# A two-layer graph network on one core: the first dense layer summed in half chunks, one norm shared between two engines, and the branch moved ahead of the stores' wait

## The reference

```python
h = relu(LN(x))
for l in 1, 2, 3:                      # SAGE, mean over incoming edges
    agg = segment_sum(h[src], dst) / count(dst)
    h = agg @ Wl.T + bl + h @ Wr.T     # relu after layers 1 and 2
x = x + h
h = relu(LN(x))
m = gelu((h[src] + edge_attr) @ We1 + be1) @ We2 + be2
u = (1 + eps) * h + segment_sum(m, dst)
x = x + gelu(u @ Wu1 + bu1) @ Wu2 + bu2
```

## Time and profile before

| what | value |
|---|---|
| median of 3 runs | 880.73 us (879.21 to 881.85) |
| profiled execution, its own time | 879.47 us |
| its span, first to last instruction | 877.3 us |
| PE busy | 826.8 us (94%), 4876 matmuls |
| DVE busy | 694.9 us (79%) |
| ACT busy | 323.8 us (37%) |
| POOL busy | 379.7 us (43%) |
| mean granted clock of PE | 0.969 |

### The profile page before, as it was taken

The page is one execution under the profiler, slowest core; times in us unless marked ns, Lnnn a source line. Parts: engine busy times, 40 slices in busy tenths (PEclk is TensorE's granted clock), DMA queues, the critical chain, the costliest instruction groups (busy, mean ns, idle before and its releaser), DMA issues.

```text
span 877.3 us, 16376 instructions
## 1 busy us (share of the span) xinstructions
PE 826.8 (94%) x4876; PEld 632.6 (72%) x4876; DVE 694.9 (79%) x1887; ACT 323.8 (37%) x570; POOL 379.7 (43%) x439
## 2 busy tenths in 40 slices
PE   3688999999999999999899999999999999999995
PEld 1243555555687787778677888888887898888884
DVE  8999999998355444454799989988979997997981
ACT  3566677776255555544211111121121112112111
POOL 1000000000022222232477777777777777777771
PEclk9569999999999999999799999999999999999998
DMA  4301011001000000011573443444443453444431
GB/s 112 120 2 13 3 15 13 14 3 15 11 1 0 1 1 12 13 32 40 131 197 106 128 137 109 134 137 149 138 139 93 147 149 94 147 138 140 128 87 33
DMA packets 38403, 67.61 MB, mean 77 GB/s; under 512 B 15178, under 2 KB 25893, under 8 KB 38054
## 3 DMA queue, kind: packets, MB, share of 16 engines
q1 hardware_dynamic: 27302, 43.95, 17.0%
q0 software_dynamic: 11008, 22.57, 9.8%
HBM read 63.18 MB, written 3.30 MB: 76 GB/s over the span
## 4 chain that ended last, share of the span: by engine, by line
PE 79%; DVE 12%; POOL 4%; issue 2%; DMA 1%; ACT 1%; SPq 0%; ACTq 0%; DVEq 0%
PE f_ps L1414 20%; PE f_ps L1359 16%; PE f_ps L1456 11%; PE f_ps L1352 10%; PE f_ps L1400 8%; POOL f_adj L678 4%; PE f_ps L1257 3%; PE f_ps L1250 2%; PE f_ps L1326 2%; DVE f_region L747 2%; DVE f_region L745 2%; PE f_ps L1396 1%; PE f_ps L1288 1%; DVE f_region L751 1%; DVE f_region L749 1%
## 5 line engine op out<-in xcount | busy, mean ns | idle before, releaser
L678 POOL DMA_INDIRECT f_adj<-table,f_by_edge x344 | 327.9, 953 | 105.8 <-issue 102.8
L970 DVE TENSOR_SCALAR f_select<-f_ps 128x512 fp32r<-128x512 f32 x425 | 261.0, 678 | 9.0 <-PE f_ps L1414 8.1
L1414 PE MATMUL f_ps<-f_select,f_pair 125*128 125x512 f32 x850 | 220.1, 407 | 4.5 <-DVE f_select L970 4.5
L663 POOL CAST f_wide<-f_adj 125x500 fp32r<-125x500 uint8 (+1 forms) x70 | 40.4, 577 | 358.5 <-ACT f_adj L1122 212.6
L1414 PEld LDWEIGHTS f_ps<-f_select,f_pair 125*128 125x128 f32 x850 | 156.7, 191 | 42.6 <-issue 7.1
L1236 ACT ACTIVATE f_adj<-f_adj 128x512 f32<-128x512 f32 (+1 forms) x88 | 55.1, 626 | 295.5 <-DVE f_adj L1092 259.1
L1359 PE MATMUL f_ps<-f_wide,f_pair 125*128 125x500 f32 (+1 forms) x700 | 162.5, 385 | 1.5 <-DVE f_wide L802 0.6
L1122 ACT CAST f_adj<-f_ps 128x500 f32 x213 | 125.9, 591 | 55.8 <-PE f_ps L1257 43.3
L1359 PEld LDWEIGHTS f_ps<-f_wide,f_pair 125*128 125x128 f32 x700 | 122.2, 189 | 33.5 <-issue 6.2
L1352 PE MATMUL f_ps<-f_adj,f_parts 125*128 125x500 fp8e4 (+1 forms) x525 | 128.7, 354 | 0.0
L1456 PEld LDWEIGHTS f_ps<-f_adj 128*128 128x128 f32 x984 | 119.4, 192 | 10.0 <-issue 9.2
(11 more groups left out here) (149 smaller groups left out, 716.0 us busy)
## 6 DMA issues: line engine op xcount, KB each, us to landing
f_region<-in_edge_attr_T SPq DMA_DIRECT2D x33, 768.0 KB
f_adj<-table SPq DMA_DIRECT2D x512, 0.5 KB
f_adj<-table,f_by_edge POOLq DMA_INDIRECT x344
f_src_rows<-in_src_row SPq DMA_DIRECT2D x16, 256.0 KB, 3.5
f_xT<-in_xT SPq DMA_DIRECT2D x1, 1562.5 KB, 6.6
f_adj<-inv SPq DMA_DIRECT2D x1, 1562.5 KB, 7.5
out<-f_xT SPq DMA_DIRECT2D x6, 250.0 KB, 3.0
table<-f_region SPq DMA_DIRECT2D x6, 224.0 KB
```

Source lines behind the costliest of these rows:

```text
L678: pool.indirect_dma_start(out=rows[:, r % RW, j * D:(j + 1) * D], out_offset=None, in_=table, in_offset=bass.IndirectOffsetOnAxis(ap=table ...
L970: ins = dve.tensor_scalar(select[:, u % SELECT, :], offset, float(b * NP - CENTRE), None, ALU.is_equal)
L1414: ins = pe.matmul(z_columns(g), chosen[0:NP, p, b, :], select[0:NP, u % SELECT, :], start=b == 0 and p == 0, stop=b == NB - 1 and p == 1, ...
```

## The change

- Each chunk of layer 1 except 0 and 6 is summed as two halves of 250 columns, each with 75 matmuls. A half may begin two slots after its own columns are filled (`half_group`: 36; 53, 70; 87, 104; 121, 138; 155, 172; 189, 206; 212). The second half need not wait for a new PSUM region.
- `rate`: 2.8 full-width units a slot before slot 80, then 2.3. The units of chunk 0 now lie in slots 38 to 64, chunk 1 in 64 to 93, 2 in 94 to 126, 3 in 126 to 159, 4 in 159 to 191, 5 in 191 to 216, 6 in 216 to 218. Full-width equivalents behind the build: 45.25 (before 81.75).
- `ready` is 24 + 5c, six slots sooner, for `norm0`, `turn`, `high` and the rest of the splitting.
- `norm0` of chunks 1, 3, 5 goes from DVE to ACT (one activation for each block, with the ReLU).
- `variance(c)` on PE also waits for the square root of the chunk before.
- Five more tiny comparisons in the check of the inputs (`small`).
- SP no longer waits for the stores inside the block; the semaphores are cleared by POOL after the flag is loaded, without the second barrier; SP waits for the stores and clears their semaphore behind the branch.

```diff
-        self.build_group = last(self.EP * self.DT)
+        self.build_group = last(self.EP * self.DT, self.node_end)
+        self.half_end = [[e for e in (self.cols(c)[0] + self.NBC // 2 * self.NP, self.node_end[c]) if c and e < self.node_end[c] or e == self.node_end[c]]
+                         for c in range(self.NC)]
+        self.half_group = [last(self.EP * self.DT, ends) for ends in self.half_end]
...
-    RATE = 2.3
+    RATE, SOONER, FIRST = 2.3, 2.8, 80
...
-            ready = 30 + 5 * c
+            ready = 24 + 5 * c
...
+    def rate(self, s, slot):
+        return self.SOONER if slot < self.FIRST else self.RATE if slot < s.GB else self.AFTER
+
     def dense(self, s):
         ends, slot, budget = [], 0, 0.0
         for n in range(LAYERS * s.NC):
-            lo, hi = s.cols(n % s.NC)
-            cost = (hi - lo) / (s.NBC * s.NP)
-            if n < s.NC:
-                slot, budget = (slot, budget) if slot > s.build_group[n] + 1 else (s.build_group[n] + 2, 0.0)
-            for b in range(s.NB):
-                for i in range(self.PARTS[n // s.NC]):
-                    while budget >= (self.RATE if slot < s.GB else self.AFTER):
-                        budget -= self.RATE if slot < s.GB else self.AFTER
-                        slot += 1
-                    budget += cost
-                    self.units.setdefault(slot, []).append((n, b, i))
+            for h, (lo, hi) in enumerate(s.halves(n) if n < s.NC else [s.cols(n % s.NC)]):
+                cost = (hi - lo) / (s.NBC * s.NP)
+                if n < s.NC and slot < s.half_group[n][h] + 2:
+                    slot, budget = s.half_group[n][h] + 2, 0.0
+                for b in range(s.NB):
+                    for i in range(self.PARTS[n // s.NC]):
+                        while budget >= self.rate(s, slot):
+                            budget -= self.rate(s, slot)
+                            slot += 1
+                        budget += cost
+                        self.units.setdefault(slot, []).append((n, b, i, h))
             ends.append(slot)
...
-            sp.wait_ge(stored, 16 * NC)
...
-                    dve.wait_ge(normed0, c + 1)
+                    wait_normed0(dve, c)
...
+            def normalise0(c):
+                if c == 1:
+                    act.wait_ge(scaled0, 2)
+                for b in s.blocks(c):
+                    ins = act.activation(x_rows[0:NP, b, :], x_rows[0:NP, b, :], ACT.Relu, bias=shift0[0:NP, b:b + 1],
+                                         scale=std0[0:NP, b:b + 1])
+                ins.then_inc(normed0_act, 1)
...
                 pe.wait_ge(squared, c + 1)
+                if c:
+                    pe.wait_ge(std_ready, c)
...
                 if l == 0:
-                    ins = pe.matmul(ps[:, dense_ps(i):dense_ps(i) + width(c)], parts1[0:NP, p, b, :],
+                    lo, hi = s.halves(c)[h]
+                    o = dense_ps(i) - s.cols(c)[0]
+                    ins = pe.matmul(ps[:, o + lo:o + hi], parts1[0:NP, p, b, :],
...
-        fast_path(nc, s, t, table, counts, inv, outT, spill)
+        fast_path(nc, s, t, table, counts, inv, outT, spill, sem, stored)
         again = nc.values_load(spill[0:1, 0:1], min_val=0, max_val=1)
+        nc.clear_and_free_semaphores(taken)
 
         with nc.If(again):
+            nc.sync.wait_ge(stored, 16 * s.NC)
+            nc.all_engine_barrier()
             for e in engines:
                 e.nop()
             general_path(nc, s, t, table, outT)
+        nc.sync.wait_ge(stored, 16 * s.NC)
+        nc.sync.sem_clear(stored)
```

More of the change, by code:

```diff
@@ L46, in __init__, with last @@
         self.node_end = [min(n_nodes, (c + 1) * self.NBC * self.NP) for c in range(self.NC)]
-        def last(per):
+        def last(per, ends):
             groups = -(-n_edges // per)
             return [groups - 1 if e == n_nodes else
-                    min(groups - 1, -(-(e + self.MARGIN) * n_edges // (n_nodes * per)) - 1) for e in self.node_end]
+                    min(groups - 1, -(-(e + self.MARGIN) * n_edges // (n_nodes * per)) - 1) for e in ends]
         self.FT = -(-n_edges // P)
@@ L102, in pieces, with halves @@
                 if max(lo, self.cols(c)[0]) < min(hi, self.node_end[c])]
+    def halves(self, c):
+        return list(zip([self.cols(c)[0]] + self.half_end[c], self.half_end[c]))
     def blocks(self, c):
@@ L170, in __init__ @@
         for slot, units in self.units.items():
-            for n, b, i in units:
+            for n, b, i, _ in units:
                 if n >= s.NC and i == 0:
@@ L226, in carve, with fast_path @@
     return v, offset + -(-n // 32) * 32
-def fast_path(nc, s, t, table, counts, inv, outT, spill):
+def fast_path(nc, s, t, table, counts, inv, outT, spill, sem, stored):
     plan = Plan(s)
@@ L461, in ordinal, with wait_normed0 @@
             return (n - NC) * NB + b
+        def wait_normed0(engine, c):
+            if c % 2:
+                engine.wait_ge(normed0_act, c // 2 + 1)
+            else:
+                engine.wait_ge(normed0, c // 2 + 1)
         def t_rows(c):
@@ L1004, in _ @@
             small = [(0, 0.0, ALU.is_gt), (NT - 1, float(N - s.DW), ALU.is_lt)]
-            small += [(s.DT * (g + 1), float(e), ALU.is_lt) for e, g in zip(s.node_end, s.build_group) if g + 1 < GB]
+            small += [(s.DT * (g + 1), float(e), ALU.is_lt) for c in range(NC)
+                      for e, g in zip(s.half_end[c], s.half_group[c]) if g + 1 < GB]
             def check_tiles():
@@ L1203, in _ @@
                     activate(i)
+                for c in plan.due("norm0", slot):
+                    if c % 2:
+                        normalise0(c)
                 for j in plan.due("high", slot):
@@ L1339, in mix_rows, with dense_unit @@
                 ins.then_inc(rows_mixed, 1)
-            def dense_unit(i, b, p):
+            def dense_unit(i, b, p, h):
                 l, c = i // NC, i % NC
-                lo, hi = s.cols(c)
                 if b == 0 and p == 0:
                     if i < NC:
-                        pe.wait_ge(kept, s.build_group[c] + 1)
-                    if i >= 2:
+                        pe.wait_ge(kept, s.half_group[c][h] + 1)
+                    if i >= 2 and h == 0:
                         pe.wait_ge(agg_kept, i - 1)
@@ L1351, in dense_unit @@
                 if l == 0:
-                    ins = pe.matmul(ps[:, dense_ps(i):dense_ps(i) + width(c)], parts1[0:NP, p, b, :],
+                    lo, hi = s.halves(c)[h]
+                    o = dense_ps(i) - s.cols(c)[0]
+                    ins = pe.matmul(ps[:, o + lo:o + hi], parts1[0:NP, p, b, :],
                                     adj[0:NP, b, lo:hi].bitcast(F8), start=b == 0 and p == 0,
-                                    stop=b == NB - 1 and p == plan.PARTS[0] - 1)
+                                    stop=b == NB - 1 and p == plan.PARTS[0] - 1, skip_group_check=True)
                 else:
@@ L1362, in dense_unit @@
                         ins.then_inc(spent, 1)
-                if b == NB - 1 and p == plan.PARTS[l] - 1:
+                if b == NB - 1 and p == plan.PARTS[l] - 1 and (l or h == len(s.halves(c)) - 1):
                     ins.then_inc(dense_done, 1)
@@ L1368, in _ @@
                     sum_group(slot)
-                for i, b, p in plan.units.get(slot, []):
-                    dense_unit(i, b, p)
+                for i, b, p, h in plan.units.get(slot, []):
+                    dense_unit(i, b, p, h)
                 for c in plan.due("cent", slot):
@@ L2021, in gnn_kernel, with sem @@
         spill = ctx.enter_context(nc.sbuf_tensor("spill", [1, 1], I32))
-        fast_path(nc, s, t, table, counts, inv, outT, spill)
+        taken = []
+        def sem(name):
+            taken.append(nc.alloc_semaphore("f_" + name))
+            return taken[-1]
+        stored = nc.alloc_semaphore("f_stored")
+        fast_path(nc, s, t, table, counts, inv, outT, spill, sem, stored)
         again = nc.values_load(spill[0:1, 0:1], min_val=0, max_val=1)
+        nc.clear_and_free_semaphores(taken)
         with nc.If(again):
+            nc.sync.wait_ge(stored, 16 * s.NC)
+            nc.all_engine_barrier()
             for e in engines:
```

13 lines of the change are left out of this document (7 added, 6 removed).

## The result

The changed kernel takes 883.63 us (median of 20 runs) where the kernel before, on the same chip in turn with it, takes 880.60 (20 runs): a ratio of 1.0031, 95% interval 1.0024 to 1.0038. It is slower by 0.3%, 2.7 us by the ratio and 3.0 by the medians. The forecast was 876.8, with a range up to 880.7; both missed. One of the 20 runs took 1050.69 us at a granted clock of 0.747 and is left out of the ratio (without it the median is 883.61). The profiled execution took 882.49 us, its span 880.7.

What follows compares the result with a forecast made beforehand. DVE was taken to set the pace up to 98.4 us, PE from there to layer 1's end near 238. Terms 1.9 - 0.7 + 2.7 = 3.9 us off the 880.73 median gave 876.8 us, range 872.6 to 880.7.

Steps and rivals of the forecast that it cites:

- the norm on ScalarE: Layer 1, odd chunks' first norm: four activations take 0.85 us a chunk (0.7 to 1.1); PE waits 1.4 us for two turns.
- TensorE's wait for the inverse counts: Layer 1, chunks 3 and 4: DVE waits 0.7 and 2.3 us for transfers, costing PE 0.8 us (0 to 2.5).
- the end of layer 3: Later cent of chunk 5 and shorter chain behind it, plus 0.2 us at adjacent turns: 0.7 us lost (-0.5 to 1.6).
- the end: Behind the last store: barrier 1.3 us and flag load 1.45 us sooner, PE's branch unchanged; 2.7 us won (1.3 to 2.8).
- PE's idle time before 98.4 us: Layer 1, slots 38 to 77: PE idle 7.2 of 43.7 us, a pool that work done sooner could fill.
- the ledger of PE's work: Slots 38 to 77: PE's work summed to 43.3 us, with waits 45.7, ending at 102.4 us, 3.5 us ahead.
- Halves: Layer 1's 250-column units: 375 additional matmuls at 0.002 us each cost 0.8 us.
- Rival (d): Weight loads no longer hide behind half-length matmuls; at 50 ns for each extra matmul, 894.8 us. Chance 0.03.
- Layer 1 together: Layer 1: 3.5 us ahead at slot 77, less 0.8 and 0.8 us, makes it 1.9 us sooner.
- (a): Rival: layer 1 gains nothing, ACT's later norm, DVE's waits and half clock eating 1.9 us; 878.7 us. Chance 0.20.
- (c): Rival: the new end doesn't pay, as drain or SP's late code delays it; gain 1.2 to 2.5, 878.9 us. Chance 0.07.
- (e): Rival: the kernel is slower for another reason, a new wait at the seams; no size given. Chance 0.02.

Runs made afterwards that it cites:

- e4: The changed kernel with ScalarE's norm given a constant scale for chunk 3 and no shift for chunk 5, chunk 1 unaltered: 881.97 us (1 run).
- e2: The changed kernel with every chunk's first norm on VectorE, still six slots sooner: 880.50 us, ratio 0.9997 to the kernel before.
- e6: The changed kernel with the counts of chunks 0 to 4 summed three slots sooner: 879.01 us, ratio 0.9983 to the kernel before.
- e3: The changed kernel with the units of layers 2 and 3 cut into slots as before the change: 881.53 us, ratio 1.001 to the kernel before.
- e7: The changed kernel with all first norms on VectorE and due from slot 30 again, as before: 882.47 us, ratio 1.0021 to the kernel before.
- e1: The kernel before with only the change's new end (stores awaited and semaphores cleared behind the flag's load): 878.88 us, ratio 0.998.
- e5: The kernel before, unchanged, profiled a second time: 881.50 us (1 run).

## Why the prediction was wrong

Four terms of the sum failed: the norm on ScalarE (priced 0.85 us a chunk, measured 1.65), TensorE's wait for the inverse counts (0.8, measured 2.4), the end of layer 3 (0.7 lost, measured some 2.2 up to the first gather) and the end (2.7 won, about 0.7 of it left in the median). The plan's idea, that PE's idle time before 98.4 us can be filled, was right, but the change as made did not fill it.

**The norm on ScalarE was priced at half of what it costs.** "For 128 columns from SBUF I take 0.20, with the end of the last 0.85 for a chunk", bounds 0.7 and 1.1: it is 1.65 us, above the upper bound. The nearest rows were activations without an operand per partition, and the bound was made from them alone. The price that the Trainium skill ("ScalarE: Activation LUTs", What ACT_TABLE_LOAD costs) states, as quoted under e4, gives an estimate of 1.64 us. With 0.8 us more a chunk, the first unit comes at 57.91 and not at 56.7, and the turns of chunks 3 and 5 wait 1.27 and 1.65 us, 2.9 for both where the prediction had 1.4. The `turn` of chunk 0 of the next layer, in slot 74, starts at 101.40; with its 0.88 and slots 75 to 77 at 0.84, 0.95 and 0.84 the units of slot 77 end at 104.9, forecast 102.4. With the norm on VectorE (e2) that `turn` starts at 97.87, 3.5 us sooner: the ledger of PE's work was right, and its pool could be filled. Instead of 3.5 us ahead, the kernel after is 1.0 ahead at slot 77 (98.4 + 7.5 - 104.9).

**The inverse counts: DVE's wait was right, its price for TensorE was not.** DVE was to wait 0.7 and 2.3 us, and waited 0.98 and 2.58. The prediction let the four groups in hand absorb it, 0.8 us (bounds 0 and 2.5). It cost 2.4 in layer 1 (e6); the median fell by 4.6, with 1.2 from the clock at the end of layer 3 and the rest not placed. That fewer than four groups were in hand when the wait began would explain it, but how many there were was not measured.

**Halves**: 0.8 us for 375 matmuls was right within what the trace resolves (0.106 us for a half, 0.21 for a whole), but by luck: the prediction's own 0.107 gives 2 x 0.107 - 0.21 = 0.004 us for each, 1.5 us, and the sum took 0.002. Rival (d), the exposed weight load, is refuted.

**Layer 1 together**: 1.0 - 0.8 - 2.4 = 2.2 us later; by the marks, with `turn` 12 taken off before, 238.75 - (238.27 - 0.87) = 1.35 later, forecast 1.9 sooner. The 0.85 between the two sums was not traced.

**The end of layer 3**: forecast 0.7 us lost. The last table store is issued 3.21 us later (429.12 against 425.91 in the earlier trace rows), 1.35 of it from layer 1, so 1.9 were lost here. `cent` begins 2.3 us later (420.03 against 417.71), so 1.0 of it is lost here, where 1.5 was forecast; from `cent` to the store it took 9.09 us and not 8.20, 0.9 more, where "about 1 us is won" was forecast. That is the step that failed: without the 13 units PE stands idle twice in this chain (418.30 to 420.03, 421.15 to 422.38) and then was granted 0.74 and 0.50 of its clock in the two windows. `variance` and `rows` took 1.48 and 1.93 us, at full clock in e3 0.82 and 0.99: 1.6 us, without which the chain would have won 0.7. The same idle stretches did not cost the same in every execution: the two steps took 3.41 us together in after and e7, 3.2 in e2, 3.0 in e4 and 2.2 in e6.

**The end**: forecast 2.7. The barriers did come 2.7 us sooner. Two things took most of it back. PE's branch is 1.07 us longer in the kernel after (4.53 against 3.46). And from the span's end to the execution's end it takes longer with the new end: over all executions with both times on record this remainder has a median of 2.0 us with the old end (102 executions, 1.6 to 2.5) and of 2.8 with the new end and whole chunks (35), 3.0 with the new end and halves (88, 1.6 to 4.5). The prediction took it as unchanged. So e1, whose branch is not longer, has a span 2.5 us shorter than the kernel before in the median (876.1 against 878.65) and a time only 1.6 shorter; in the kernel after some 2.7 - 1.1 - 0.9 = 0.7 are left. Its profiled execution hides this, being one with a short remainder (1.79 us, median 2.91): from the last DVE end to the execution's end it took 7.72 us, where before took 9.86, 2.1 less. What the engines do in that remainder no trace shows.

**The sum.** At the first gather the kernel after is 3.56 us later than before (431.49 against 427.93), where 1.2 sooner was forecast: 3.25 of the difference from layer 1, 1.5 from the end of layer 3. With 2.0 lost at the end this makes 6.8 of the 6.9 us between -3.9 and +3.0. This puts marks of single executions beside medians, and e5's first gather is 0.25 us sooner than before's, so that it closes only to some tenths. The gather stage is left out: it took 443.28 us in after, between the 441.68 and the 443.86 of the same code in the two profiles of before.

**The rivals.** None had the whole. (a) named the norm and DVE's waits, "ACT's later norm, DVE's waits and half clock eat the 1.9 us", but let them eat the gain and no more. Its clock was at the wrong place for most of the loss: what the low clock cost was at the end of layer 3. In layer 1, by the durations of matmuls, PE's pace rose between 58.0 and 59.7 us before and between 59.8 and 62.3 us after, so the low clock did last somewhat longer; what that cost was not separated. (c), "the end doesn't pay", was right in part, with 0.7 left of 2.7. (e), slower for a new wait at the seams, with a chance of 0.02, had the sign.

## What to carry to other kernels

When a sum is moved ahead, list everything else that it reads, with the slot in which each is ready: this change lost on a transfer that came three slots too late, and one number in the plan turned +0.3% into -0.2%. A step that several engines wait for is not to be put on the engine with the most idle time without its own duration there: here 1.65 us for four blocks, against 1.10 on VectorE; and an operation with operands that no row shows is bounded by rows that have such operands, or is left with an open bound. Work that seems merely late at the end of a stage may be what holds TensorE's clock up for the chain behind it. And where the end of a program is changed, compare the time behind the last instruction of the span too, over many executions: a single profile showed the gain and not what it lost there.

## What the runs showed of the hardware

An activation of 125 x 128 f32 costs 0.095 us more for each operand that has a value per partition, four in a row 1.27 us with one and 1.65 with two. The transposes of a chunk took 1.09 us at 48 us and 0.65 from 62 us on, although the recorded clock is 1.00 from 20 us on in the kernel after; the recorded clock of a window is not proof of the pace in it. The branch at the program's end takes TensorE 3.3 to 4.5 us and the four other engines 0.05 to 0.07; TensorE's is 4.2 to 4.5 us in the nine profiles of kernels with the 375 additional matmuls ahead of it, 3.3 to 3.8 in the seven without. With the semaphores' clear and SP's wait for the stores moved behind the flag's load, the time from the span's end to the execution's end is 0.8 to 1.0 us longer in the median. One and the same code ran its gather stage in 441.7 us in one execution and in 443.9 in the next.
